# Rounding of two ternary weights in a feed-forward layer: one engine for both, or VectorE for the first and GpSimd for the second

## The chip, the cores and the metric

The kernel runs on one core of a Trainium2 chip as one program on five engines: TensorE (PE), VectorE (DVE), ScalarE (ACT), GpSimd (POOL) and SyncE (SP, which here only starts DMAs). Times are device microseconds of one execution. The metric is the median of several executions; lower is better.

## The reference

Two layers of gated cross attention and feed-forward over x (2 x 512 tokens, width 512). The last of the four blocks is the one that matters here: a feed-forward block whose activations are rounded to 8 bits and whose two weights are rounded to the three values -1, 0 and 1, times a scale.

```python
def _weight_quant(w):
    scale = 1.0 / jnp.clip(jnp.mean(jnp.abs(w)), EPS, None)
    return jnp.clip(jnp.round(w * scale), -1.0, 1.0) / scale

def _bitlinear(x, w, b):                      # w1: 2048 x 512, w2: 512 x 2048
    return jnp.einsum('bsd,hd->bsh', _act_quant(x), _weight_quant(w)) + b

h = gelu(_bitlinear(x, w1, b1))
x = x + tanh(g_ffn[1]) * _bitlinear(h, w2, b2)
```

The mean is over the whole weight, so no piece of a weight can be rounded before all of it has been read and summed.

## The kernel before

The program is written out by hand: every stage appends a function to the list of each engine, an engine runs its functions in order, and engines meet only through semaphores. The stage of interest is `bit_ffn`, the last one, which starts when the second cross attention has added its last block to x.

Its setup has these steps. Both weights are loaded as float32 (`raw[0]`, `raw[1]`, each 128 partitions x 8192). ScalarE sums their absolute values (`sizes`, L2685). TensorE adds the sums over the partitions (L2738), and VectorE makes the mean and its inverse (`wmean`, `winv`, L2584 and L2586). Each weight is then treated in four pieces of 128 x 2048, CH = 4:

- two VectorE operations on a piece in place: times the inverse mean, at most 1 (L2592), and then at least -1, plus a large number that makes the addition round (MAGIC, L2594). The second waits for the first through a semaphore.
- one ScalarE operation, which takes MAGIC off and writes bfloat16 (L2694, into `wq`).

ScalarE takes the eight pieces in a fixed order, the four of the first weight and then the four of the second. After all eight it copies its share of the transposed weights: TensorE transposes both weights in 16 groups (L2753; eight groups per weight), and the groups are copied out of PSUM by ScalarE (even groups, L2678) and VectorE (odd groups, L2676) in turn. There are four PSUM buffers for groups, so TensorE's fifth group waits until ScalarE has copied the first. The groups of the first weight wait for its four rounded pieces (`s_wq` at CH), those of the second for all eight.

Behind that come, for each pair of token tiles, normalisation and rounding on VectorE, `hidden` (L2774), GELU, a second rounding, and the output matmuls (L2795). These wait for all 16 groups. GpSimd has nothing to do in this stage.

Of the kernel before, what the change touches and what calls it, by code (L numbers as in the profile page):

```python
# [14 lines left out]
ALU = mybir.AluOpType  # L15
ACT = mybir.ActivationFunctionType
# [32 lines left out]
def program(nc, a, out):  # L49
    ctx = ExitStack()  # L50
    with ctx:
        def sem(name):
            return ctx.enter_context(nc.semaphore(name))

        def keep(name, shape, dt=F32):
            return ctx.enter_context(nc.sbuf_tensor(name, shape, dt))
# [7 lines left out]
        ident = keep("ident", [P, P])  # L64
# [14 lines left out]
        programs = {"SP": [], "ACT": [], "PE": [], "DVE": [], "POOL": []}  # L79
# [89 lines left out]
        def sb(name, shape, dt=F32):  # L169
            return phase.enter_context(nc.sbuf_tensor(name, shape, dt))  # L170
# [2333 lines left out]
        def bit_ffn():  # L2504
# [4 lines left out]
            MAGIC = 1.5 * 2.0 ** 23  # L2509
            TOP, BOTTOM = 127.0, -128.0  # L2510
            GROUPS = 8
            raw = [sb("f_raw1", [P, HC, D]), sb("f_raw2", [P, KC, HID])]
            wq = [sb("f_wq1", [P, HC, D], BF16), sb("f_wq2", [P, KC, HID], BF16)]
            w1T, w2T = sb("f_w1T", [P, KC, HID], BF16), sb("f_w2T", [P, HC, D], BF16)
            identb, ones = sb("f_identb", [P, P], BF16), sb("f_ones", [P, P])
            size, wmean, winv = sb("f_size", [P, 2]), sb("f_wmean", [P, 2]), sb("f_winv", [P, 2])
# [13 lines left out]
            WTB = [pairs[2 + i // 2][:, (i % 2) * BANK:(i % 2 + 1) * BANK].bitcast(BF16) for i in range(4)]  # L2530

            s_w = [sem("f_w1"), sem("f_w2")]
            s_b, s_id, s_one = [sem(f"f_{n}") for n in ("b", "id", "one")]
            s_size, s_sum, s_mean, s_wc, s_wr, s_wq, s_wt, s_wa, s_wd = [
                sem(f"f_{n}") for n in ("size", "sum", "mean", "wc", "wr", "wq", "wt", "wa", "wd")]
            s_ch, s_r, s_q, s_tr, s_te, s_m1, s_z, s_g, s_m2, s_o, s_x2 = [
# [1 line left out]
            CH = 4  # L2538
# [20 lines left out]
            def chunk(t3, k):  # L2559
                n = t3.shape[1] // CH  # L2560
                return t3[:, k * n:(k + 1) * n, :]
# [13 lines left out]

            def vector(dve):
                dve.wait_ge(*x2_done)
                dve.memset(ones[:, :], 1.0).then_inc(s_one, 1)

                dve.memset(scrap[:, 36:37], 0.0).then_inc(s_z, HB)  # L2580
                dve.memset(scrap[:, 37:38], 0.0).then_inc(s_o, 2)

                dve.wait_ge(s_sum, 1)
                dve.tensor_scalar(wmean[:, :], HID_B[0][:, 0:2], 1.0 / (HID * D), LEAST, ALU.mult, ALU.max).then_inc(s_mean, 1)  # L2584
                dve.wait_ge(s_mean, 1)
                dve.reciprocal(winv[:, :], wmean[:, :]).then_inc(s_mean, 1)  # L2586
                dve.wait_ge(s_mean, 2)

                for w in range(2):
                    for k in range(CH):  # L2590
                        c = chunk(raw[w], k)
                        dve.tensor_scalar(c, c, winv[:, w:w + 1], 1.0, ALU.mult, ALU.min).then_inc(s_wc, 1)  # L2592
                        dve.wait_ge(s_wc, w * CH + k + 1)
                        dve.tensor_scalar(c, c, -1.0, MAGIC, ALU.max, ALU.add).then_inc(s_wr, 1)  # L2594
                for g in range(1, 2 * GROUPS, 2):
                    dve.wait_ge(s_wt, g + 1)
                    turned(dve, g)
                dve.wait_ge(s_rstd, 4)
                dve.wait_ge(s_b, 32)

                steps = 0

                def step(ins, i):

                    nonlocal steps
                    steps += 1
                    ins.then_inc(s_ch, 1)

                    dve.wait_ge(s_ch, steps if i is None else first("steps", i) + steps)

                def quantise(src, n, w, i):
                    m, q = most[:, n:n + 1], scale[:, n:n + 1]
                    step(dve.tensor_scalar(m, m, LEAST, None, ALU.max), i)
                    step(dve.reciprocal(q, m), i)
                    step(dve.tensor_scalar(q, q, TOP, None, ALU.mult), i)
                    step(dve.tensor_scalar(unscale[:, n:n + 1], m, 1.0 / TOP, wmean[:, w:w + 1], ALU.mult, ALU.mult), i)
                    step(dve.tensor_scalar(src, src, q, MAGIC, ALU.mult, ALU.add), i)
                    dve.tensor_scalar(src, src, MAGIC + TOP, MAGIC + BOTTOM, ALU.min, ALU.max).then_inc(s_r, 1)

                def tile(t):  # L2620

                    if isinstance(t, int):
                        return x3[:, t, :], mv[:, 2 * t:2 * t + 1], rstd[:, t:t + 1]
                    return x3[:, bass.ds(t, 1), :].rearrange("p t d -> p (t d)"), mv[:, bass.ds(t * 2, 1)], rstd[:, bass.ds(t, 1)]

                def norm(pair, i):
                    for s in range(2):
                        xt, mean, one_over = tile(pair * 2 + s)
                        step(dve.tensor_scalar(h[s][:, :], xt, mean, one_over, ALU.subtract, ALU.mult), i)
                        step(dve.tensor_reduce(most[:, s:s + 1], h[s][:, :], AX.X, ALU.max, apply_absolute_value=True), i)  # L2630
                        quantise(h[s][:, :], s, 0, i)

                def hidden(pair, s):
                    for k in range(HB):
                        dve.wait_ge(s_m1, 2 * HB * pair + HB * s + k + 1)
                        cols = slice(k * BANK, (k + 1) * BANK)
                        dve.scalar_tensor_tensor(z[s][:, cols], HID_B[k][:, :], unscale[:, s:s + 1], b1[:, cols],
                                                 ALU.mult, ALU.add).then_inc(s_z, 1)

                norm(0, None)  # L2640
                for s in range(2):
                    hidden(0, s)
                norm(1, None)

                def body(i):
                    nonlocal steps
                    steps = 0
                    for s in range(2):
                        dve.wait_ge(s_g, 2 * i + s + 1)
                        step(dve.tensor_reduce(most[:, 2 + s:3 + s], z[s][:, :], AX.X, ALU.max, apply_absolute_value=True), i)  # L2650
                        quantise(z[s][:, :], 2 + s, 1, i)
                    for s in range(2):
                        if ahead(i, 1):
                            dve.wait_ge(s_q, first("rounded", i) + s + 1)
                            hidden(i + 1, s)
                        dve.wait_ge(s_m2, 2 * i + s + 1)
                        dve.scalar_tensor_tensor(o[s][:, :], OUT_B[s][:, :], unscale[:, 2 + s:3 + s], b2[:, :],
                                                 ALU.mult, ALU.add).then_inc(s_o, 1)
                        dve.wait_ge(s_o, 2 * i + s + 3)
                        xt = tile(i * 2 + s)[0]  # L2660
                        dve.scalar_tensor_tensor(xt, o[s][:, :], tgate[:, 3:4], xt, ALU.mult, ALU.add).then_inc(s_x2, 1)
                    if ahead(i, 2):
                        norm(i + 2, i)

                iterations(dve, body)

            def turned(engine, g):

                src = WTB[g % 4][:, :]
                if g < GROUPS:  # L2670
                    dst = w1T[:, g // 2, (g % 2) * 8 * P:(g % 2 + 1) * 8 * P]
                else:
                    m = (g - GROUPS) * 2
                    dst, src = w2T[:, m:m + 2, :], src.rearrange("p (m d) -> p m d", m=2)
                if g % 2:
                    engine.tensor_copy(dst, src).then_inc(s_wd, 1)  # L2676
                else:
                    engine.activation(dst, src, ACT.Copy).then_inc(s_wa, 1)  # L2678
# [7 lines left out]

            def scalar(act):
                act.wait_ge(s_size, 2)
                act.activation(identb[:, :], ident[:, :], ACT.Copy).then_inc(s_id, 1)
                act.activation(scrap[:, 40:41], eps[:, 0:1], ACT.Copy).then_inc(s_te, 2)  # L2690
                for w in range(2):
                    for k in range(CH):
                        act.wait_ge(s_wr, w * CH + k + 1)
                        act.activation(chunk(wq[w], k), chunk(raw[w], k), ACT.Copy, bias=-MAGIC).then_inc(s_wq, 1)  # L2694
                for g in range(0, 2 * GROUPS, 2):
                    act.wait_ge(s_wt, g + 1)
# [36 lines left out]
                iterations(act, body)  # L2733

            def tensor(pe):
                pe.wait_ge(s_one, 1)
                pe.wait_ge(s_size, 2)
                pe.matmul(HID_B[0][:, 0:2], ones[:, :], size[:, :], start=True, stop=True).then_inc(s_sum, 1)  # L2738
                pe.wait_ge(s_id, 1)
                for g in range(2 * GROUPS):  # L2740
                    if g < GROUPS:
                        pe.wait_ge(s_wq, CH)
# [62 lines left out]
            programs["DVE"].append(vector)  # L2805
            programs["ACT"].append(scalar)
            programs["PE"].append(tensor)

        bit_ffn()
        phase.close()  # L2810

# [69 lines left out]
```

## Time and profile before

| | |
|---|---|
| median of three executions | 2995.21 us (2987.34 to 2997.44) |
| the profiled execution: its time | 2988.46 us |
| the profiled execution: span of the trace | 2986.4 us |
| busy share of the span: PE, DVE, ACT, POOL | 81%, 60%, 49%, 37% |
| the stage `bit_ffn` in the trace | 2792.8 us to the end |

Clock times below are microseconds from the start of the trace. The rows further down come from the profile's page and from views of the trace: time windows with the busy time of each engine, the chain of work that ended last, the timeline of one engine, the statistics of one line of code, and groups of instructions by shape.

### The profile page before, as it was taken

How to read it: one execution, taken by the hardware profiler on the slowest of the kernel's cores; microseconds unless marked ns; L12 is line 12 of the kernel's file. 1: busy time of each engine (PE TensorE's matmuls, PEld its weight loads, DVE VectorE, ACT ScalarE, POOL GpSimd, SP SyncE). 2: the span in 40 equal slices, each digit the busy share in tenths (PEclk: the TensorE clock that was granted, in tenths of full speed). 3: DMA queues.
4: the chain of work that ended last, by engine and by line, in shares of the span. 5: the costliest groups of instructions: out<-in, count | busy, mean ns of one | idle time of the engine just before them, and what ended most of it. 6: DMA issues, size and time to landing. Idle time of an engine off the chain costs nothing.

```text
span 2986.4 us, 46041 instructions
## 1 busy us (share of the span) xinstructions
PE 2409.3 (81%) x14781; PEld 2001.7 (67%) x14789; DVE 1789.4 (60%) x3820; ACT 1472.2 (49%) x3029; POOL 1093.7 (37%) x1483
## 2 busy tenths in 40 slices
PE   6999999999958988889974899898057488889355
PEld 3878787878747888888863888887045376767232
DVE  3555555555544666666644554554467587878576
ACT  3444444444435666666642333332035586777543
POOL 0232323232304444444422656554454354444000
PEclk9999999999978999999985999999579799999787
DMA  3000000000000000000003455453626642331100
GB/s 107 19 18 11 7 18 18 11 7 18 0 29 11 19 18 18 18 18 18 18 11 108 154 174 176 156 175 113 185 77 219 169 99 68 80 86 64 74 8 21
DMA packets 111034, 195.02 MB, mean 65 GB/s; under 512 B 18336, under 2 KB 54432, under 8 KB 109024
## 3 DMA queue, kind: packets, MB, share of 16 engines
q1 hardware_dynamic: 97392, 159.59, 17.3%
q0 software_dynamic: 6640, 21.76, 2.2%
q10 hardware_dynamic: 6912, 12.59, 1.1%
q8 instruction: 42, 0.69, 0.1%
q14 instruction: 48, 0.39, 0.0%
HBM read 149.87 MB, written 44.04 MB: 65 GB/s over the span
## 4 chain that ended last, share of the span: by engine, by line
PE 66%; DVE 13%; issue 8%; ACT 7%; POOL 2%; DMA 2%; SPq 1%; DVEq 0%; ACTq 0%; POOLq 0%
PE pair L1768 8%; PE pair L535 6%; PE pair L1784 5%; PE pair L1066 5%; PE pair L1116 4%; PE pair L563 4%; PE pair L2453 4%; PE pair L496 4%; PE pair L521 3%; PE pair L1138 3%; PE pair L2436 3%; PE pair L2465 2%; PE pair L1100 2%; PE pair L552 2%; PE pair L502 2%
## 5 line engine op out<-in xcount | busy, mean ns | idle before, releaser
L433 ACT ACTIVATE x_p<-x_p,x_least 128x1024 f32<-128x1024 f32 x128 | 147.2, 1150 | 307.7 <-DVE x_least L389 307.7
L1440 POOL TENSOR_TENSOR e_w<-e_raw,e_w 128x2048 fp32r<-128x2048 f32 x48 | 220.4, 4593 | 153.7 <-ACT e_w L1406 153.6
L373 DVE TENSOR_TENSOR x_pT<-pair,x_pT 128x512 fp32r<-128x512 f32 x256 | 164.3, 684 | 121.2 <-ACT x_pT L452 121.2
L1768 PE MATMUL pair<-m_h,e_w 128*128 128x320 f32 x1536 | 229.5, 310 | 2.7 <-POOL e_w L1440 2.7
L1768 PEld LDWEIGHTS pair<-m_h,e_w 128*128 128x128 f32 x1536 | 228.0, 189 | 4.5 <-issue 3.1
L467 POOL TENSOR_TENSOR x_carry<-x_rtotal 128x1 f32<-128x1 f32 x128 | 24.9, 195 | 558.3 <-DVE x_rtotal L366 558.3
L535 PE MATMUL pair<-x_pT,x_v 128*128 128x256 f32 x1536 | 208.3, 292 | 9.2 <-DVE x_pT L373 9.2
L2365 DVE TENSOR_REDUCE z_most<-pair 128x1 f32<-128x1008 f32 x128 | 153.9, 1203 | 95.7 <-PE pair L2475 78.9
L535 PEld LDWEIGHTS pair<-x_pT,x_v 128*128 128x128 f32 x1536 | 192.7, 193 | 26.4 <-issue 18.4
L563 PE MATMUL pair<-x_kT,x_qT 128*128 128x512 f32 x768 | 207.3, 405 | 0.0
L978 ACT ACTIVATE s_p<-s_p,s_least 128x128 f32<-128x128 f32 (+3 forms) x256 | 143.6, 561 | 123.4 <-DVE s_least L888 123.4
L1116 PE MATMUL pair<-s_pT,s_v 128*128 128x256 f32 (+1 forms) x1152 | 158.9, 284 | 47.6 <-DVE s_pT L865 47.6
L2401 ACT ACTIVATE z_p<-pair,z_most 128x1008 f32<-128x1008 f32 (+1 forms) x256 | 174.6, 697 | 40.8 <-DVE z_most L2366 40.8
L1116 PEld LDWEIGHTS pair<-s_pT,s_v 128*128 128x128 f32 x1152 | 153.3, 196 | 60.0 <-issue 30.8
L2436 PE MATMUL pair<-ident,z_p 128*128 128x128 f32 x1024 | 144.7, 281 | 51.7 <-DVE z_pT L2358 50.7
L2387 ACT ACTIVATE z_pT<-pair 128x512 fp32r<-128x512 f32 x256 | 141.6, 601 | 88.6 <-PE pair L2436 88.6
L2436 PEld LDWEIGHTS pair<-ident,z_p 128*128 128x128 f32 x1024 | 117.2, 143 | 90.7 <-DVE z_pT L2358 62.1
L1038 POOL TENSOR_TENSOR s_carry<-s_rtotal 128x1 f32<-128x1 f32 x256 | 50.1, 196 | 345.9 <-DVE s_rtotal L859 345.6
L2421 POOL TENSOR_SCALAR z_p<-z_p,z_rtotal 128x1008 f32<-128x1008 f32 (+1 forms) x256 | 175.1, 697 | 0.0
L865 DVE TENSOR_TENSOR s_pT<-pair,s_pT 128x128 fp32r<-128x128 f32 (+3 forms) x256 | 124.6, 487 | 81.6 <-ACT s_pT L964 81.5
L2358 DVE TENSOR_TENSOR z_pT<-pair,z_pT 128x512 fp32r<-128x512 f32 x256 | 162.8, 677 | 4.8 <-ACT z_pT L2387 3.9
L452 ACT ACTIVATE x_pT<-pair 128x512 fp32r<-128x512 f32 x256 | 138.2, 593 | 43.7 <-PE pair L521 43.7
(322 smaller groups left out, 6112.6 us busy)
## 6 DMA issues: line engine op xcount, KB each, us to landing
e_raw<-in_L_ffn_w SPq DMA_DIRECT2D x48, 1024.0 KB
y_rows<-hslot ACTq DMA_DIRECT2D x48, 256.0 KB, 4.6
z_v<-z_vst SPq DMA_DIRECT2D x16, 768.0 KB, 3.6
z_kS<-z_k SPq DMA_DIRECT2D x24, 512.0 KB, 10.4
z_vS<-z_v SPq DMA_DIRECT2D x8, 1536.0 KB, 6.7
f_raw<-in_L_ffn_w SPq DMA_DIRECT2D x2, 4096.0 KB, 13.5
z_qS<-z_q SPq DMA_DIRECT2D x24, 256.0 KB, 4.5
s_wraw<-in_L_ffn_wq SPq DMA_DIRECT2D x9, 512.0 KB, 4.3
```

The costliest lines, as they stand in the source:

```text
L373: dve.tensor_tensor(pT[1][:, keys, q * P:(q + 1) * P], TR[j][:, :].rearrange("p (k n) -> p k n", n=P), pT[0][:, keys, q * P:(q + 1) * P].b ...
L535: mm = pe.matmul(OB[:, cols], v[x0][b][:, k, :], pT[x1][:, k, cols], start=(half == 0 and n == 0 and k == 0), stop=(half == 1 and n == 2 a ...
L563: mm = pe.matmul(SC[n % 2][:, j * BANK:(j + 1) * BANK], qT[x0][b][n // QT][:, n % QT * P:(n % QT + 1) * P], kT[x1][b][:, j * BANK:(j + 1) ...
L1066: mm = pe.matmul(o[:, 0:PW], hTa[x0][:, c, rows], w[x1][:, c, :], start=(n == 0 and c == 0), stop=(n == 2 and c == KC - 1))
L1116: mm = pe.matmul(OB[:, cols], v[b][:, k, first:first + 2, :].rearrange("p k d -> p (k d)"), pT[x1][:, k, cols], start=(i % 2 == 0 and half ...
L1440: pool.tensor_tensor(dst[1][:, :, :], raw[parity][:, :, :], dst[0][:, :, :].bitcast(F32), ALU.subtract).then_inc(s_lo, 1)
L1768: mm = pe.matmul(GU[m % 2][:, j * BANK:j * BANK + CAP], w[x0][:, c, m * P:(m + 1) * P], XS[s][x1][:, c, :], start=(n == 0 and c == 0), sto ...
L2358: dve.tensor_tensor(pT[1][:, k, cols], TR[i][:, :].rearrange("p (k n) -> p k n", n=P), pT[0][:, k, cols].bitcast(F32), ALU.subtract).then_ ...
L2365: dve.tensor_reduce(most[:, w, 0:1], SC[n % 2][:, 0:MAIN], AX.X, ALU.max, negate=True)
L2401: act.activation(p[w][:, cols], SC[n % 2][:, cols], ACT.Exp, bias=most[:, w, k:k + 1], accum_out=total[:, w, k:k + 1]).then_inc(s_ex, 1)
L2421: pool.tensor_scalar(p[w][:, cols], p[w][:, cols], rtotal[:, w, k:k + 1], 1.0, ALU.mult, ALU.mult).then_inc(s_pn, 1)
L2436: mm = pe.transpose(TR[i][:, k * P:(k + 1) * P], p[n % RING][:, kk * P:(kk + 1) * P], ident[:, :])
```

## The change

VectorE keeps the two operations on the four pieces of the first weight. The same two operations on the four pieces of the second weight are given to GpSimd, in a new function at the end of its program, with two semaphores of its own (`s_pc` between the two operations of a piece, `s_pr` for ScalarE). GpSimd starts when the inverse means are there, which is when VectorE starts too. ScalarE's order of pieces stays; only the semaphore that it waits for differs for the last four.

Two semaphores are saved by counting on others: the memset of `ones` now counts on `s_mean` (whose later values grow by one), and ScalarE's copy of the identity counts on `s_size`.

```diff
-                dve.memset(ones[:, :], 1.0).then_inc(s_one, 1)
+                dve.memset(ones[:, :], 1.0).then_inc(s_mean, 1)
...
-                for w in range(2):
-                    for k in range(CH):
-                        c = chunk(raw[w], k)
-                        dve.tensor_scalar(c, c, winv[:, w:w + 1], 1.0, ALU.mult, ALU.min).then_inc(s_wc, 1)
-                        dve.wait_ge(s_wc, w * CH + k + 1)
-                        dve.tensor_scalar(c, c, -1.0, MAGIC, ALU.max, ALU.add).then_inc(s_wr, 1)
+                for k in range(CH):
+                    c = chunk(raw[0], k)
+                    dve.tensor_scalar(c, c, winv[:, 0:1], 1.0, ALU.mult, ALU.min).then_inc(s_wc, 1)
+                    dve.wait_ge(s_wc, k + 1)
+                    dve.tensor_scalar(c, c, -1.0, MAGIC, ALU.max, ALU.add).then_inc(s_wr, 1)
...
+            def gpsimd(pool):
+                pool.wait_ge(s_mean, 3)
+                for k in range(CH):
+                    c = chunk(raw[1], k)
+                    pool.tensor_scalar(c, c, winv[:, 1:2], 1.0, ALU.mult, ALU.min).then_inc(s_pc, 1)
+                    pool.wait_ge(s_pc, k + 1)
+                    pool.tensor_scalar(c, c, -1.0, MAGIC, ALU.max, ALU.add).then_inc(s_pr, 1)
...
-                        act.wait_ge(s_wr, w * CH + k + 1)
+                        act.wait_ge((s_wr, s_pr)[w], k + 1)
...
-                pe.wait_ge(s_one, 1)
+                pe.wait_ge(s_mean, 1)
...
-                pe.wait_ge(s_id, 1)
+                pe.wait_ge(s_size, 3)
...
+            programs["POOL"].append(gpsimd)
```

GpSimd's instructions at the end of its program, as a difference with what each waits for left out. The first two rows are the last of the cross attention stage; `f_raw` is `raw` and `f_winv` is `winv`.

```order
 L2421 TENSOR_SCALAR z_p<-z_p,z_rtotal 128x1008
 L2421 TENSOR_SCALAR z_p<-z_p,z_rtotal 128x16
+L2670 TENSOR_SCALAR f_raw<-f_raw,f_winv 128x2048
+L2672 TENSOR_SCALAR f_raw<-f_raw 128x2048
+L2670 TENSOR_SCALAR f_raw<-f_raw,f_winv 128x2048
+L2672 TENSOR_SCALAR f_raw<-f_raw 128x2048
+L2670 TENSOR_SCALAR f_raw<-f_raw,f_winv 128x2048
+L2672 TENSOR_SCALAR f_raw<-f_raw 128x2048
+L2670 TENSOR_SCALAR f_raw<-f_raw,f_winv 128x2048
+L2672 TENSOR_SCALAR f_raw<-f_raw 128x2048
```

Eight operations are added behind everything else that GpSimd does, and nothing stands behind them.

ScalarE's instructions from its sums to the first copies of transposed groups, before:

```order
1161 L2685 ACTIVATE f_wq,f_size<-f_raw 128x8192 [waits f_w1,x_wd]
1162 L2685 ACTIVATE f_wq,f_size<-f_raw 128x8192 [waits f_w2]
1163 L99 ACT_TABLE_LOAD [waits ln_mv]
1164 L99 ACTIVATE std<-mv,eps 128x8 [waits s_eps]
1165 L2689 ACTIVATE f_identb<-ident 128x128 [waits f_size]
1166 L2690 ACTIVATE scrap<-eps 128x1
1167 L2694 ACTIVATE f_wq<-f_raw 128x2048 [waits f_wr] x8
1168 L2678 ACTIVATE f_w1T<-pair 128x1024 [waits f_wt] x4
```

and the same place of the changed kernel:

```order
1161 L2692 ACTIVATE f_wq,f_size<-f_raw 128x8192 [waits f_w1,x_wd]
1162 L2692 ACTIVATE f_wq,f_size<-f_raw 128x8192 [waits f_w2]
1163 L99 ACT_TABLE_LOAD [waits ln_mv]
1164 L99 ACTIVATE std<-mv,eps 128x8 [waits s_eps]
1165 L2696 ACTIVATE f_identb<-ident 128x128 [waits f_size]
1166 L2697 ACTIVATE scrap<-eps 128x1
1167 L2701 ACTIVATE f_wq<-f_raw 128x2048 [waits f_wr] x4
1168 L2701 ACTIVATE f_wq<-f_raw 128x2048 [waits f_pr] x4
1169 L2685 ACTIVATE f_w1T<-pair 128x1024 [waits f_wt] x4
```

The eight conversions stand where they stood, ahead of the first copy of a transposed group; the last four now wait for GpSimd's semaphore.

## Rows read from the trace of the kernel before

**Rows 1.** Windows: each engine's busy time, clock granted to PE, DMA share.

```profile
core 0: us, PE busy (x) PEld busy (x) DVE busy (x) ACT busy (x) POOL busy (x), PEclk, DMA share, GB/s
2816.00:2836.00 20.00, 3.57 (x32) 3.33 (x32) 19.70 (x17) 13.57 (x8) 0.00 (x0) 0.50 0.00 0
2836.00:2847.00 11.00, 7.92 (x96) 7.77 (x96) 4.69 (x8) 9.14 (x9) 0.00 (x0) 0.65 0.00 0
2842.00:2846.00 4.00, 4.00 (x59) 3.99 (x57) 2.25 (x4) 3.10 (x4) 0.00 (x0) 0.78 0.00 0
```

**Rows 2.** The chain that ended last, from the rounding on: start, us, what.

```profile
2816.03 1.30 DVE f_raw L2592
2817.35 1.23 DVE f_raw L2594
...
2834.55 1.24 DVE f_raw L2594
2835.79 0.02 issue
2835.81 1.91 ACT f_wq L2694
2837.72 0.92 ACT f_w1T L2678
2838.64 0.14 issue
2838.78 1.23 PE pair L2753 x10
```

**Rows 3.** Timeline of the same stretch: start, us, instruction, [idle before and releaser].

```profile
2825.98 1.91 ACT L2694 ACTIVATE f_wq<-f_raw 128x2048 bf16<-128x2048 f32 x1 [0.55 <-DVE f_raw L2594]
2828.04 3.57 PE L2753 MATMUL pair<-f_identb,f_wq 128*128 128x128 bf16 x32 [12.44 <-ACT f_wq L2694]
2837.63 1.92 ACT L2678 ACTIVATE f_w1T<-pair 128x1024 bf16<-128x1024 bf16 x2
```

**Rows 4.** Statistics of the pieces' lines: ns min/median/max, first and last start.

```profile
L2592 DVE TENSOR_SCALAR f_raw<-f_raw,f_winv x8: 1279/1281/1285, 2816.0 to 2833.2; 128x2048 f32<-128x2048 f32 x8
L2594 DVE TENSOR_SCALAR f_raw<-f_raw x8: 1226/1227/1228, 2817.3 to 2834.6; 128x2048 f32<-128x2048 f32 x8
```

**Rows 5.** GpSimd's groups by shape: busy us, mean ns, idle before.

```profile
L1440 POOL TENSOR_TENSOR e_w<-e_raw,e_w 128x2048 fp32r<-128x2048 f32 x48 | 220.4, 4593 | 153.7 <-ACT e_w L1406 153.6
L468 POOL TENSOR_SCALAR x_p<-x_p,x_rtotal 128x1024 f32<-128x1024 f32 x128 | 144.0, 1125 | 0.0
L1039 POOL TENSOR_SCALAR s_p<-s_p,s_rtotal 128x512 f32<-128x512 f32 x64 | 44.9, 701 | 0.0
```

**Rows 6.** Timelines of DVE and of POOL, 2168 to 2182, second cross attention.

```profile
2169.00 3.35 DVE L2082 TENSOR_TENSOR z_wkvraw<-z_wkvraw,z_wmean 128x1024 f32<-128x1024 f32 x1
2174.64 4.94 DVE L2082 TENSOR_TENSOR z_bd<-z_bd,z_wmean 128x512 f32<-128x512 f32 x1
...
2168.92 2.35 POOL L2243 TENSOR_TENSOR z_wd<-z_wdraw,z_wd 128x1024 fp32r<-128x1024 f32 x1 [37.38 <-ACT z_wd L2169]
2171.23 3.34 POOL L2243 TENSOR_TENSOR z_wd<-z_wdraw,z_wd 128x1024 fp32r<-128x1024 f32 x1
2174.53 4.49 POOL L2250 TENSOR_TENSOR z_cT<-z_xThi,z_cT 128x2048 fp32r<-128x2048 f32 x1
```

**Rows 7.** One line's statistics, then timelines of DVE and POOL at 2247.

```profile
L2132 DVE TENSOR_SCALAR hslot<-x,mv,rstd x8: 534/1608/1612, 2242.4 to 2282.3; 128x512 f32<-128x512 f32 x8
...
2245.83 0.25 DVE L2156 RECIPROCAL z_rdev<-z_dev 128x16 f32<-128x16 f32 x1
2247.14 1.61 DVE L2132 TENSOR_SCALAR hslot<-x,mv,rstd 128x512 f32<-128x512 f32 x1
...
2246.16 1.05 POOL L2259 TENSOR_TENSOR z_kt<-z_kt,z_rdev 128x512 f32<-128x512 f32 x1 [4.24 <-DVE z_rdev L2156]
2247.17 1.30 POOL L2266 TENSOR_TENSOR z_vst<-z_vt,z_vst 128x512 fp32r<-128x512 f32 x1
```

**Rows 8.** Statistics of two lines, then timelines at 908.9, self attention's start.

```profile
L1021 POOL TENSOR_TENSOR s_rot<-s_raw,s_cos x64: 872/881/1164, 902.6 to 1477.8; 128x320 f32<-128x320 f32 x64
L814 DVE TENSOR_TENSOR s_turned<-s_raw,s_sin x2: 491/818/1146, 908.9 to 909.3; 128x320 f32<-128x320 f32 x2
...
908.90 1.55 DVE L814 TENSOR_TENSOR s_turned<-s_raw,s_sin 128x320 f32<-128x320 f32 x2 [2.56 <-ACT s_raw L928]
...
908.94 1.16 POOL L1021 TENSOR_TENSOR s_rot<-s_raw,s_cos 128x320 f32<-128x320 f32 x1 [1.23 <-ACT s_raw L928]
909.31 1.15 DVE L814 TENSOR_TENSOR s_turned<-s_raw,s_sin 128x320 f32<-128x320 f32 x1
```

More of the change, by code:

```diff
@@ L2532, in bit_ffn @@
             s_w = [sem("f_w1"), sem("f_w2")]
-            s_b, s_id, s_one = [sem(f"f_{n}") for n in ("b", "id", "one")]
+            s_b, s_pc, s_pr = [sem(f"f_{n}") for n in ("b", "pc", "pr")]
             s_size, s_sum, s_mean, s_wc, s_wr, s_wq, s_wt, s_wa, s_wd = [
@@ L2584, in vector @@
                 dve.tensor_scalar(wmean[:, :], HID_B[0][:, 0:2], 1.0 / (HID * D), LEAST, ALU.mult, ALU.max).then_inc(s_mean, 1)
-                dve.wait_ge(s_mean, 1)
+                dve.wait_ge(s_mean, 2)
                 dve.reciprocal(winv[:, :], wmean[:, :]).then_inc(s_mean, 1)
-                dve.wait_ge(s_mean, 2)
-                for w in range(2):
-                    for k in range(CH):
-                        c = chunk(raw[w], k)
-                        dve.tensor_scalar(c, c, winv[:, w:w + 1], 1.0, ALU.mult, ALU.min).then_inc(s_wc, 1)
-                        dve.wait_ge(s_wc, w * CH + k + 1)
-                        dve.tensor_scalar(c, c, -1.0, MAGIC, ALU.max, ALU.add).then_inc(s_wr, 1)
+                dve.wait_ge(s_mean, 3)
+                for k in range(CH):
[3 more added lines that the diff above has]
+                    dve.tensor_scalar(c, c, -1.0, MAGIC, ALU.max, ALU.add).then_inc(s_wr, 1)
                 for g in range(1, 2 * GROUPS, 2):
@@ L2688, in scalar @@
                 act.wait_ge(s_size, 2)
-                act.activation(identb[:, :], ident[:, :], ACT.Copy).then_inc(s_id, 1)
+                act.activation(identb[:, :], ident[:, :], ACT.Copy).then_inc(s_size, 1)
                 act.activation(scrap[:, 40:41], eps[:, 0:1], ACT.Copy).then_inc(s_te, 2)
```

## Prediction

> **What bounds the kernel now.** I read the windows first, to see which engine fills the stage that is edited. From 2816 to 2836 VectorE is busy 19.70 of 20 us, ScalarE 13.57, and GpSimd not at all [rows 1]. The chain of work that ended last says the same: it runs through VectorE's sixteen operations on the weights, from 2816.03 to 2835.79, then through ScalarE's eighth conversion (1.91 us, to 2837.72), its first copy of a transposed group, and TensorE's fifth group at 2838.78 [rows 2]. So every microsecond by which ScalarE's eighth conversion ends earlier or later moves the end of the kernel, as long as the copies and transposes behind it keep their spacing. They do: TensorE's first four groups need 3.57 us and wait at 2828.04 for the fourth conversion, long before ScalarE's first copy at 2837.63 [rows 3].
>
> The quantity to work out is therefore one number: when the eighth conversion ends, against 2837.72.
>
> **What is removed.** VectorE loses eight operations, four of 1.281 and four of 1.227 us [rows 4], half of the 19.76 us that the sixteen take on the chain.
>
> **What is added.** GpSimd gets eight operations of 128x2048. The trace has none of that size, and none with min, max or add in this form. Its operations of the same form with two multiplications take 701 ns for 512 columns and 1125 ns for 1024 [rows 5]: 424 ns for 512 columns, 0.83 ns a column, so 1125 + 848 = 1973 ns for 2048, an estimate. The upper bound is the two-input subtraction of 128x2048, 4593 ns [rows 5]. I take 1.97 us, since that row has the same form; ends for the range are 1.97 and 4.59.
>
> The Trainium skill (GPSIMD Engine Reference, section 3.1) gives 1.03 cycles a column, at 1.2 GHz, to bodies with up to two operations. By the page that is an estimate of 1.76 us for one operation, and the sum below would be about 1.7 us smaller.
>
> **What VectorE and GpSimd do to each other.** This decides the case. Three places in the trace have both at work on SBUF.
>
> At 2169 VectorE's 128x1024 operation starts 0.08 us behind one of GpSimd. It takes 3.35 us: it ends at 2172.35, 1.08 us after GpSimd's ends at 2171.27. GpSimd's next, of the same size as its first, takes 3.34 instead of 2.35 us, 0.99 more. At 2174.64 a 128x512 operation of VectorE starts beside a GpSimd operation that ends at 2179.02, and ends only 0.56 us after it [rows 6]. They don't slow each other in proportion: one stands still until the other has finished.
>
> The rounding operations are of another kind on VectorE, with one input; 2048 columns in 1.23 us is 0.60 ns a column [rows 4]. Such an operation at 2247 takes 1.61 us beside GpSimd, against 0.534 for the fastest of the eight, and ends at 2248.75, 0.28 after GpSimd's at 2248.47 [rows 7]. So this kind stands still too. There GpSimd went from one of its operations (to 2247.21) to the next at 2247.17 although VectorE's had started at 2247.14; it had stood for under 0.1 us.
>
> Who is served next? At 908.90 VectorE has two operations with no wait between them (491 and 1146 ns). GpSimd's arrives 0.04 us after the first. It takes 1.16 instead of 0.88 us, so it waited about 0.28, for the first one only; the second, started at 909.31, ends at 910.46, 0.36 after GpSimd's at 910.10 [rows 8]. The two at 2169 show it the other way round: VectorE's operation gets in between two of GpSimd [rows 6]. The engine that has stood waiting for most of an operation gets the next turn, so two engines with full queues alternate strictly.
>
> **The sum.** Operation D0 of VectorE starts at 2816.03 [rows 2]. GpSimd starts about 0.08 us behind its releaser, as at 2246.16 after 2246.08 [rows 7], so VectorE is first. A VectorE operation of 1.23 to 1.28 us makes GpSimd wait about 0.99 us (the 1024-column case, whose 1.08 us after GpSimd's end is nearest to what I expect of one of these [rows 6]). GpSimd's consecutive starts are 0.04 us closer than its durations (2168.92 + 2.35 against 2171.23 [rows 6]). One turn of both is 1.97 - 0.04 + 0.99 = 2.92 us.
>
> - GpSimd's first ends at 2816.12 + 1.0 + 1.97 = 2819.1, its eighth 7 x 2.92 = 20.4 later, at 2839.5.
> - VectorE's eighth ends 1.1 us after GpSimd's seventh (2836.6), at 2837.7. The first weight, which now has only four pieces, is rounded later than both weights were before (2835.79).
> - ScalarE converts the first weight's last piece from 2837.7 to 2839.6. Only then does it come to the second weight, whose four pieces are ready by then: their starts are 1.82 us apart when nothing is waited for (2835.81 to 2837.63 [rows 2, 3]), so the eighth conversion starts at 2839.6 + 3 x 1.82 = 2845.1 and ends at 2847.0.
>
> Against 2837.72 that is +9.3 us. The profiled execution would go from 2988.46 (span 2986.4) to 2997.8. That execution lies 6.75 us under the median of the three, 2995.21, so I add the difference to the median: **3004.5 us**, +0.31%.
>
> The rest costs nothing. TensorE's first groups start at about 2839.6 instead of 2828.04, take 3.57 us, and are done before ScalarE's first copy at 2846.9; with a cover of 3.7 us gone they would cost what lies beyond. VectorE's odd copies of them come under the same cover. The merged semaphores count the same events. PE's clock is at 0.50 before these transposes and 0.78 in 2842 to 2846 [rows 1]; a shorter gap between the two bursts of transposes might let it rise earlier, worth under 1 us of the 7.92 [rows 1], which I leave out. GpSimd has nothing behind the eight, and no DMA moves.
>
> The Trainium skill (SBUF — State Buffer, section "Who interferes with whom") says that GpSimd and such VectorE operations share a port pair under an exclusive lock, held for a whole instruction. The trace agrees, with 1.61 against 0.534 us; it speaks against this change, since work that alternates is a sum, and not a maximum.
>
> **Rivals.**
>
> *GpSimd's operations are slower with min, max and add (30%).* The turn grows by what they take over 1.97. With 4.59: the eighth ends at 2816.12 + 1.0 + 4.59 + 7 x 5.54 = 2860.5; ScalarE, after VectorE's last at 2856 or so, converts at 2857, 2859, 2861, 2863 and 2865, and ends at about 2866.5: +28.8, 3024. For it: the same engine needs 2.24 ns a column for the subtraction [rows 5]. Against: that one reads two tensors, this one reads one.
>
> *VectorE gets two in a row where no wait lies between them (13%).* Then the order is D0, G0, D1 D2, G1, D3 D4, G2, D5 D6, G3, D7 and four of GpSimd alone. VectorE is done at about 2832.3, GpSimd at 2840.0, and the last conversion ends at 2841.9: +4.2, 2999.4, no measurable change. Against: the two at 908.90 were parted [rows 8].
>
> *No exclusion between operations of these kinds (8%).* This is the case on the other side of no change. VectorE's pieces keep their spacing, ScalarE ends the fourth at 2827.89 (2825.98 + 1.91 [rows 3]), GpSimd ends its eighth at 2816.1 + 8 x 1.93 = 2831.6, so ScalarE runs through: 2827.8 + 3 x 1.82 + 1.91 = 2835.2, -2.5 us, 2992.7. More than that can't be gained, since ScalarE's conversions then bound the stage. It decides once the two overlap for over half of the time. Against: 0.534 against 1.61 us [rows 7].
>
> *Anything else (7%):* a different first turn, or a shift elsewhere by timing alone.
>
> **How the numbers follow.** Strict alternation at 1.97 us has 42%, and gives the time predicted, 3004.5. The range, 2996 to 3025, takes in the doubled turns below and the slow GpSimd operations above; it leaves out no exclusion and the tails. 0.3% is 9.0 us, about what a measurement of this kernel tells from no change, and the likeliest case lies on that line: I count half of its 42% as slower, with the 30% of the slow GpSimd operations and 2% of the rest: slower 0.53. Same: 21 + 13 + 8 + 2 = 0.44. Faster 0.03.
>
> **What would show it.** In the changed profile, VectorE's eight operations should take about 3.0 us each but the first, and GpSimd's eight 2.9 to 3.0; their ends should alternate; ScalarE's fifth conversion should start near 2839.6, right behind its fourth, and its eighth end near 2847. The prediction is wrong if VectorE's operations keep 1.23 to 1.28 us, if GpSimd's take well over 3 us, or if TensorE's fifth group is not moved by the shift of the eighth conversion.

## The result and the profile after

The changed kernel takes 3037.74 us (median of four, 3034.66 to 3039.0) against 2992.03 us (four executions, 2987.34 to 2997.44): a ratio of 1.0151, 95% interval 1.0129 to 1.0172. It is 45.7 us slower. The forecast was 9.3 us slower, with a range that ended at 3025.

GpSimd's timeline of the changed kernel, from the moment when the inverse means are there (start, duration, instruction):

```profile
2816.51 8.26 POOL L2670 TENSOR_SCALAR f_raw<-f_raw,f_winv 128x2048 f32<-128x2048 f32 x1 [43.25 <-DVE f_winv L2586]
2824.85 7.94 POOL L2672 TENSOR_SCALAR f_raw<-f_raw 128x2048 f32<-128x2048 f32 x1
2832.78 8.11 POOL L2670 TENSOR_SCALAR f_raw<-f_raw,f_winv 128x2048 f32<-128x2048 f32 x1
...
2873.21 7.93 POOL L2672 TENSOR_SCALAR f_raw<-f_raw 128x2048 f32<-128x2048 f32 x1
```

The chain of work that ended last, same stretch (start, us, what), answers to [rows 2]:

```profile
2816.45 1.30 DVE f_raw L2591
2817.75 0.02 issue
2817.77 8.08 DVE f_raw L2593
2825.85 8.03 DVE f_raw L2591
...
2866.14 8.08 DVE f_raw L2593
2874.21 0.02 issue
2874.24 9.11 ACT f_wq L2701 x5
2883.34 0.92 ACT f_w1T L2685
2884.26 0.14 issue
2884.39 1.65 PE pair L2760 x14
```

Two things are to be seen. The order is the one that was forecast: VectorE's first operation runs alone in 1.30 us, and each further one ends about a microsecond after one of GpSimd's (2824.77, then 2825.85); the first weight's fourth piece comes late; and ScalarE then runs five conversions in one go. But a turn of both engines is 8.06 us, not 2.92. The eighth conversion ends at 2883.35, 66.9 us after VectorE's first start, where before it was 21.7 (2837.72 less 2816.03 [rows 2]). These 45.2 us are the loss, and nearly all of it; from VectorE's first start to the end of the trace it is 216.15 against 170.37 us, 45.8 more.

The statistics of the four lines, where [rows 4] had 1281 and 1227 ns:

```profile
L2591 DVE TENSOR_SCALAR f_raw<-f_raw,f_winv x4: 1286/8096/8100, 2816.4 to 2858.0; 128x2048 f32<-128x2048 f32 x4
L2670 POOL TENSOR_SCALAR f_raw<-f_raw,f_winv x4: 8107/8107/8256, 2816.5 to 2865.0; 128x2048 f32<-128x2048 f32 x4
L2593 DVE TENSOR_SCALAR f_raw<-f_raw x4: 8065/8066/8077, 2817.8 to 2866.1; 128x2048 f32<-128x2048 f32 x4
L2672 POOL TENSOR_SCALAR f_raw<-f_raw x4: 7929/7930/7939, 2824.8 to 2873.2; 128x2048 f32<-128x2048 f32 x4
```

They read as if both engines had become slow. One has, as the second experiment below shows: the other's durations hold its standing still.

### The profile page after: what moved, and what is told of

The parts are those of the page before. It is cut to its first block, busy times and chain, and to the rows that moved or that the text cites. A ratio compares the mean times of both kernels' runs of the same rounds, so it can differ in the third digit from the quotient of the medians.

```text
span 3032.6 us, 46049 instructions
## 1 busy us (share of the span) xinstructions
PE 2410.8 (79%) x14789; PEld 2002.2 (66%) x14789; DVE 1829.0 (60%) x3812; ACT 1471.3 (49%) x3029; POOL 1153.6 (38%) x1491
## 4 chain that ended last, share of the span: by engine, by line
PE 65%; DVE 15%; issue 8%; ACT 7%; DMA 2%; POOL 2%; SPq 1%; DVEq 0%; ACTq 0%; POOLq 0%
PE pair L1768 7%; PE pair L535 6%; PE pair L1784 5%; PE pair L1066 5%; PE pair L563 4%; PE pair L1116 4%; PE pair L2453 4%; PE pair L496 4%; PE pair L521 3%; PE pair L1138 3%; PE pair L2436 3%; PE pair L2465 2%; PE pair L1100 2%; PE pair L552 2%; PE pair L502 2%
## 5 line engine op out<-in xcount | busy, mean ns | idle before, releaser
L452 ACT ACTIVATE x_pT<-pair 128x512 fp32r<-128x512 f32 x256 | 138.2, 594 | 45.2 <-PE pair L521 45.2
```

## The experiments

Three theories could explain 8 us for a GpSimd operation. The diffs below leave lines out at "...". **K**: the pair of arithmetic operations decides, and those with min, max and add go a slow way. **C**: VectorE's operations beside it slow GpSimd down. **S**: 2048 columns are slow whatever the kind.

### Only the kinds changed

This kernel leaves out the rounding of the second weight.

```diff
-                    pool.tensor_scalar(c, c, winv[:, 1:2], 1.0, ALU.mult, ALU.min).then_inc(s_pc, 1)
+                    pool.tensor_scalar(c, c, winv[:, 1:2], 1.0, ALU.mult, ALU.mult).then_inc(s_pc, 1)
...
-                    pool.tensor_scalar(c, c, -1.0, MAGIC, ALU.max, ALU.add).then_inc(s_pr, 1)
+                    pool.tensor_scalar(c, c, 1.0, 1.0, ALU.mult, ALU.mult).then_inc(s_pr, 1)
```

> GpSimd's eight operations in the changed kernel are all two multiplications (first by the inverse mean and 1.0, second by 1.0 and 1.0), so the second weight is scaled but not rounded; shape, place and order are unchanged. Theory K (the kinds of operations decide): each takes about 1.97 us alone and 2.96 us with its wait for VectorE, VectorE's from the second on about 3.0 us, the eighth conversion of ScalarE ends near 2847 and the time is 9 to 10 us over that of before. Theory C (VectorE's operations beside it slow GpSimd) and theory S (2048 columns are slow in any kind): GpSimd's stay at 8 us and the time stays about 45 us over.

Measured: ratio 1.0043 (1.0029 to 1.0057), 3000.2 against 2987.94 us. GpSimd's timeline:

```profile
2816.82 3.06 POOL L2670 TENSOR_SCALAR f_raw<-f_raw,f_winv 128x2048 f32<-128x2048 f32 x1 [42.98 <-DVE f_winv L2586]
2819.97 2.74 POOL L2672 TENSOR_SCALAR f_raw<-f_raw 128x2048 f32<-128x2048 f32 x1
2822.69 2.93 POOL L2670 TENSOR_SCALAR f_raw<-f_raw,f_winv 128x2048 f32<-128x2048 f32 x1
```

and ScalarE's last stretch of conversions:

```profile
2838.21 9.11 ACT L2701 ACTIVATE f_wq<-f_raw 128x2048 bf16<-128x2048 f32 x5 [3.83 <-DVE f_raw L2593]
```

The eighth conversion ends at 2847.32, 30.6 us after VectorE's first start (2816.76). The prediction's sum, made for 1.97 us an operation, had 2847.0 less 2816.03, or 31.0. So with fast operations the rest of the sum holds; shape, size and the company of VectorE are the same as in the changed kernel, which speaks against C and S. (To the end of the trace the loss is 7.2 us, 177.5 against 170.4 from VectorE's first start, where the stage loses 8.9: what follows the stage differs by a microsecond or two between traces.)

### The two engines kept apart

```diff
                 pool.wait_ge(s_mean, 3)
+                pool.wait_ge(s_wr, CH)
```

> GpSimd starts its eight operations only when VectorE has done its eight, so the two never overlap. Theory K: VectorE's take 1.23 to 1.28 us, GpSimd's 7.1 and 6.9 us (8.11 and 7.93 less the 1.0 us of VectorE's turn), so the last conversion ends at about 2826 + 56 + 2 = 2884, and the time is within 2 us of that of the changed kernel, 46 us over before: the taking of turns costs almost nothing there. Theory C: GpSimd's take about 2 us, the last conversion ends near 2844 and the time is 6 us over before.

Measured: ratio 1.0162 (1.0144 to 1.0181), 3037.73 us, the same as the changed kernel. VectorE's last operation and GpSimd's first two:

```profile
2828.58 1.23 DVE L2593 TENSOR_SCALAR f_raw<-f_raw 128x2048 f32<-128x2048 f32 x1
```

```profile
2829.97 7.16 POOL L2671 TENSOR_SCALAR f_raw<-f_raw,f_winv 128x2048 f32<-128x2048 f32 x1 [53.02 <-DVE f_raw L2593]
2837.22 7.09 POOL L2673 TENSOR_SCALAR f_raw<-f_raw 128x2048 f32<-128x2048 f32 x1
```

VectorE is back at its old durations, and GpSimd takes 7.16 and 7.09 us with no rounding on VectorE beside it. Theory C is out. Of the 8.11 us in the changed kernel, 0.95 were VectorE's turn.

ScalarE's eighth conversion:

```profile
2887.33 1.91 ACT L2702 ACTIVATE f_wq<-f_raw 128x2048 bf16<-128x2048 f32 x1 [12.42 <-POOL f_raw L2673]
```

It ends 69.4 us after VectorE's first start (2819.88). Side by side it was 66.9, so with slow kinds the overlap is worth 2.5 us of the stage, though the two medians don't tell the kernels apart.

### Kinds of operation, one by one

Behind the last block of x, on a weight that nobody reads any more, each operation waits for the one before:

```diff
+                pool.wait_ge(s_x2, NT)
+                c, c5, one = raw[1][:, 0, :], raw[1][:, 0, 0:512], ones[:, 0:1]
...
+                one_more(pool.tensor_scalar(c, c, one, 1.0, ALU.mult, ALU.mult))
+                one_more(pool.tensor_scalar(c, c, one, 1.0e30, ALU.mult, ALU.min))
+                one_more(pool.tensor_scalar(c, c, -1.0e30, 0.0, ALU.max, ALU.add))
...
```

> The kernel before with the merged semaphores, and, when the last block of x is done, 14 GpSimd operations one after another on a weight that nobody reads any more: eleven kinds of 128x2048 and three of 128x512. The time is longer by their sum. Theory K: two multiplications take 1.97 us, (mult, min) 7.1, (max, add) 6.9; the others tell which kinds are slow; at 512 columns (mult, mult) takes 0.70 us and (mult, min) 1.7 to 1.9. Theory S: all of 2048 columns are alike at 7 us, and those of 512 are alike at 0.7 us. Theory C: all of 2048 columns are alike at 2 us.

Measured in one execution of 3054.51 us, GpSimd's timeline. The lines are in this order: L2814 (mult, mult), L2815 (mult, min), L2816 (max, add), L2817 (mult, max), L2818 (mult, add), L2820 (add, add), L2821 (min, max), L2822 one multiplication alone; L2825 (mult, mult) and L2826 (mult, min) on 512 columns.

```profile
2987.21 1.97 POOL L2814 TENSOR_SCALAR f_raw<-f_raw,f_ones 128x2048 f32<-128x2048 f32 x1 [209.06 <-DVE x L2661]
2989.28 7.16 POOL L2815 TENSOR_SCALAR f_raw<-f_raw,f_ones 128x2048 f32<-128x2048 f32 x1
2996.53 7.09 POOL L2816 TENSOR_SCALAR f_raw<-f_raw 128x2048 f32<-128x2048 f32 x1
3003.71 7.17 POOL L2817 TENSOR_SCALAR f_raw<-f_raw,f_ones 128x2048 f32<-128x2048 f32 x1
3010.97 1.97 POOL L2818 TENSOR_SCALAR f_raw<-f_raw,f_ones 128x2048 f32<-128x2048 f32 x1
...
3015.02 7.10 POOL L2820 TENSOR_SCALAR f_raw<-f_raw 128x2048 f32<-128x2048 f32 x1
3022.20 1.89 POOL L2821 TENSOR_SCALAR f_raw<-f_raw 128x2048 f32<-128x2048 f32 x1
3024.19 5.45 POOL L2822 TENSOR_SCALAR f_raw<-f_raw,f_ones 128x2048 f32<-128x2048 f32 x1
...
3040.64 0.69 POOL L2825 TENSOR_SCALAR f_raw<-f_raw,f_ones 128x512 f32<-128x512 f32 x1
3041.43 2.00 POOL L2826 TENSOR_SCALAR f_raw<-f_raw,f_ones 128x512 f32<-128x512 f32 x1
```

Theory K stands, and S is out: 512 columns show the same split. The constants aren't the cause: (mult, min) takes 7.16 us here with 1.0e30 on ones, and 7.16 in the run before this one with 1.0 on the real scale. The slow way costs (7.16 - 2.00) / 1536 = 3.36 ns a column, the fast one (1.97 - 0.69) / 1536 = 0.83. The two kinds that the change uses are both slow. No run shows why a pair is slow.

### More kinds

> As e3_pool_kinds, with eight other kinds of GpSimd operation on 128x2048 behind the last block of x. The theory is now that a few pairs have a fast form (1.9 to 2.0 us, as mult-mult, mult-add, min-max) and every other pair goes a slow way (7.1 us). If what counts is which two operations are paired, in either order, (add, mult) and (max, min) are fast; if the order counts, they take 7.1 us. (subtract, mult) and (mult, subtract) are open; (add, min), (min, min) and (min, add) are expected at 7.1; a plain copy at 1.9 or less.

Measured in one execution of 3036.32 us, in the order L2814 (add, mult), L2815 (max, min), L2816 (subtract, mult), L2817 (mult, subtract), L2819 (min, min), L2821 a plain copy:

```profile
2979.83 1.90 POOL L2814 TENSOR_SCALAR f_raw<-f_raw 128x2048 f32<-128x2048 f32 x1 [208.75 <-DVE x L2661]
2981.82 7.08 POOL L2815 TENSOR_SCALAR f_raw<-f_raw 128x2048 f32<-128x2048 f32 x1
2988.98 7.11 POOL L2816 TENSOR_SCALAR f_raw<-f_raw 128x2048 f32<-128x2048 f32 x1
2996.19 7.17 POOL L2817 TENSOR_SCALAR f_raw<-f_raw,f_ones 128x2048 f32<-128x2048 f32 x1
...
3010.62 7.08 POOL L2819 TENSOR_SCALAR f_raw<-f_raw 128x2048 f32<-128x2048 f32 x1
...
3024.93 1.89 POOL L2821 COPY f_raw<-f_raw 128x2048 f32<-128x2048 f32 x1
```

Neither of the two simple rules holds: (add, mult) is fast as (mult, add) is, but (max, min) is slow where (min, max) is fast. Of fourteen pairs tried, four are fast: mult-mult, mult-add, add-mult and min-max. The other two pairs of this run, (add, min) and (min, add), took 7.10 and 7.08 us. Most pairs were timed once, in one execution; (mult, min) and (max, add) recur with the same durations in the second experiment, (mult, add) and (min, max) in the one with fast kinds kept apart.

### The same rounding in fast kinds

```diff
-                    pool.tensor_scalar(c, c, winv[:, 1:2], 1.0, ALU.mult, ALU.min).then_inc(s_pc, 1)
+                    pool.tensor_scalar(c, c, winv[:, 1:2], MAGIC, ALU.mult, ALU.add).then_inc(s_pc, 1)
...
-                    pool.tensor_scalar(c, c, -1.0, MAGIC, ALU.max, ALU.add).then_inc(s_pr, 1)
+                    pool.tensor_scalar(c, c, MAGIC + 1.0, MAGIC - 1.0, ALU.min, ALU.max).then_inc(s_pr, 1)
```

> The changed kernel, with GpSimd's two operations written with the kinds that took 1.97 and 1.89 us: times the inverse mean, plus MAGIC (mult, add), then at most MAGIC + 1, at least MAGIC - 1 (min, max). The values are those of the reference: rounded first, then clipped. Theory K with strict turns: GpSimd's operations 2.7 to 3.1 us, VectorE's 2.9, the eighth conversion ends 30.5 us after VectorE's first start (21.7 before, 66.9 in the changed kernel), and the time is 9 to 12 us over before, as with the two multiplications.

Measured: ratio 1.0029 (1.0018 to 1.004), 2997.11 against 2989.1 us. VectorE's first operation, GpSimd's last, and ScalarE's last five conversions:

```profile
2815.39 1.29 DVE L2591 TENSOR_SCALAR f_raw<-f_raw,f_winv 128x2048 f32<-128x2048 f32 x1
2835.83 2.74 POOL L2672 TENSOR_SCALAR f_raw<-f_raw 128x2048 f32<-128x2048 f32 x1
2836.85 9.11 ACT L2701 ACTIVATE f_wq<-f_raw 128x2048 bf16<-128x2048 f32 x5 [3.83 <-DVE f_raw L2593]
```

The eighth conversion ends 30.6 us after VectorE's first start (2845.96 less 2815.39). Rewriting two operations takes 36 of the 45 us off; what is left, 8.9 us in the stage, is what the prediction had worked out as 9.3.

### Fast kinds, the two engines kept apart

The edit is that of the second experiment, on top of the last one.

> As e5_fast_kinds, but GpSimd starts only when VectorE's eight operations are done: no overlap. If turns are exclusive, running the two side by side gains nothing over this: GpSimd's eight end at 9.9 + 8 x 2.0 = 26 us after VectorE's first start (24 when side by side), and since ScalarE converts the first weight meanwhile, the eighth conversion ends at 28, which is 2 to 3 us before that of e5_fast_kinds. Without exclusion it would end 7 us after it.

Measured: ratio 1.0021 (1.0011 to 1.0031), 2994.99 us. The eighth conversion ends 28.1 us after VectorE's first start, 2.5 us before that of the kernel in which both work at the same time:

```profile
2824.49 1.23 DVE L2593 TENSOR_SCALAR f_raw<-f_raw 128x2048 f32<-128x2048 f32 x1
```

```profile
2825.88 1.98 POOL L2671 TENSOR_SCALAR f_raw<-f_raw,f_winv 128x2048 f32<-128x2048 f32 x1 [53.24 <-DVE f_raw L2593]
...
2840.08 1.89 POOL L2673 TENSOR_SCALAR f_raw<-f_raw 128x2048 f32<-128x2048 f32 x1
```

```profile
2842.01 1.91 ACT L2702 ACTIVATE f_wq<-f_raw 128x2048 bf16<-128x2048 f32 x1 [2.14 <-POOL f_raw L2673]
```

Side by side is worse here than one behind the other, but not because the overlap gains nothing. It brings GpSimd's last operation forward, to 23.2 us after VectorE's first start (2838.57 less 2815.39) from 26.2 (2841.97 less 2815.80). But it holds up the first weight, which ScalarE needs first: five conversions then lie behind VectorE's last operation, where here a single one lies behind GpSimd's. With the slow kinds it was the other way round (66.9 side by side, 69.4 apart). It also shows what the 8.9 us of the last kernel are made of: 6.4 (28.1 less 21.7) remain without any overlap, since GpSimd needs 1.9 to 2.0 us where VectorE needed 1.2 to 1.3. Between the two ratios the intervals overlap; the difference is read from the stage.

### One piece for GpSimd

VectorE keeps seven pieces, GpSimd has the last one, in fast kinds. The loop is shown against that of the kernel before.

```diff
-                    for k in range(CH):
+                    for k in range(CH - w):
...
+                c = chunk(raw[1], CH - 1)
+                pool.tensor_scalar(c, c, winv[:, 1:2], MAGIC, ALU.mult, ALU.add).then_inc(s_pc, 1)
+                pool.wait_ge(s_pc, 1)
+                pool.tensor_scalar(c, c, MAGIC + 1.0, MAGIC - 1.0, ALU.min, ALU.max).then_inc(s_pr, 1)
```

> VectorE keeps seven pieces and GpSimd takes only the last piece of the second weight, in the fast kinds. If turns are exclusive, any operation given to GpSimd costs VectorE 1.9 us of standing still and saves it 1.23: its seventh piece is done 14 x 1.23 + 2 x 1.9 = 21.0 us after its start instead of 17.3, and the eighth conversion ends 21.0 + 1.9 + 1.8 = 24.7 us after VectorE's start, 3 us later than before. If there were no exclusion, ScalarE would end the eighth at 17.3 + 3.7 = 21.0, 0.7 us earlier than before. By time either is within 0.3% of before; the trace tells.

Measured: ratio 1.0005 (0.9995 to 1.0015). VectorE's timeline, and ScalarE's last two conversions:

```profile
2815.30 1.29 DVE L2592 TENSOR_SCALAR f_raw<-f_raw,f_winv 128x2048 f32<-128x2048 f32 x1
2816.62 2.88 DVE L2594 TENSOR_SCALAR f_raw<-f_raw 128x2048 f32<-128x2048 f32 x1
2819.43 2.90 DVE L2592 TENSOR_SCALAR f_raw<-f_raw,f_winv 128x2048 f32<-128x2048 f32 x1
2822.37 1.23 DVE L2594 TENSOR_SCALAR f_raw<-f_raw 128x2048 f32<-128x2048 f32 x1
...
2835.91 3.71 ACT L2701 ACTIVATE f_wq<-f_raw 128x2048 bf16<-128x2048 f32 x2 [0.55 <-DVE f_raw L2594]
```

Two of GpSimd's operations lengthen two of VectorE's, by 1.65 and 1.62 us, and the next is back at 1.23. The eighth conversion ends 24.3 us after the first start (2839.62 less 2815.30), 2.6 us later than before, not 0.7 earlier. Two operations cost VectorE 3.27 us of standing still, less than the 3.8 expected, and save it 2.51 (1.28 and 1.23). So VectorE's last one ends 0.8 us later (20.6 against 19.8 after the first start); the other 1.8 are a conversion, since ScalarE takes GpSimd's piece last and then has two left behind VectorE. By that price per operation no share pays while VectorE has operations waiting beside it. That is worked out from this run: one piece and four were run, and no other order of ScalarE's pieces.

### The merged semaphores alone

```diff
-                dve.memset(ones[:, :], 1.0).then_inc(s_one, 1)
+                dve.memset(ones[:, :], 1.0).then_inc(s_mean, 1)
...
-                pe.wait_ge(s_id, 1)
+                pe.wait_ge(s_size, 3)
```

> The kernel before with only the two merged semaphores; VectorE keeps all sixteen operations. All theories: no change beyond 0.3%, the eighth conversion ends within 0.5 us of 2837.7. If the merged counting had a part in the loss, it would show here as more than 1 us.

Measured: ratio 0.9998 (0.9988 to 1.0008). They cost nothing. The eighth conversion ends at 2838.72 and not within 0.5 us of 2837.7, but VectorE's first operation starts later too, at 2817.03; the distance is 21.7 us in both kernels. The shift comes from ahead of VectorE's first operation, whose start lies between 2815.30 and 2820.09 in the traces of this document.

### A version without GpSimd

The stage is shortened where it is long: ScalarE scales and rounds five of the pieces itself, and the conversions behind VectorE are gone. The diff is against the changed kernel.

```diff
+                act.wait_ge(s_mean, 3)
+                for w, k in TAKEN:
+                    act.activation(chunk(wq[w], k), chunk(raw[w], k), ACT.Identity, scale=winv[:, w:w + 1],
+                                   bias=offset[:, 0:1]).then_inc(s_wr, 1)
...
+                        dve.tensor_scalar(q, q, SMALL + 1.0, SMALL - 1.0, ALU.min, ALU.max).then_inc(s_wq, 1)
...
+                        dve.tensor_scalar(c, c, winv[:, w:w + 1], 1.0, ALU.mult, ALU.min).then_inc(s_wc, 1)
+                        dve.wait_ge(s_wc, own)
+                        dve.tensor_scalar(q, c, -1.0, SMALL, ALU.max, ALU.add).then_inc(s_wq, 1)
...
-                    engine.tensor_copy(dst, src).then_inc(s_wd, 1)
+                    engine.tensor_scalar(dst, src, -SMALL, None, ALU.add).then_inc(s_wd, 1)
```

> A version meant to beat both. The rounding is done by writing bfloat16 at 192 plus the value, where neighbours are 1 apart, and 192 is taken off where the transposed groups are copied out of PSUM. ScalarE scales and rounds five pieces by itself (1.9 us each), VectorE clips those in bfloat16 and does three pieces alone; GpSimd does nothing, and the eight conversions are gone. ScalarE is done after 5 x 1.85 = 9.3 us, VectorE after 6 x 1.25 + 5 clips of 0.7 to 1.2 us = 11 to 13.5 us, so the first copy by ScalarE of a transposed group starts near 9.5 us after VectorE's first start instead of 21.6, and TensorE's last groups wait for VectorE at 11 to 13.5: 8 to 11 us faster than before, ratio 0.996 to 0.9975. If ScalarE's scaled form is slower than its plain one, or the copies with the subtraction are, it is less.

Measured: ratio 0.9947 (0.9933 to 0.996), 2975.25 against 2989.1 us. VectorE's first clip in bfloat16, ScalarE's five pieces, and its first copies of transposed groups:

```profile
2822.55 0.69 DVE L2599 TENSOR_SCALAR f_wq<-f_wq 128x2048 bf16<-128x2048 bf16 x1
```

```profile
2820.09 10.04 ACT L2703 ACTIVATE f_wq<-f_raw,f_offset,f_winv 128x2048 bf16<-128x2048 f32 x5 [1.17 <-DVE f_winv L2590]
2830.03 1.91 ACT L2688 ACTIVATE f_w1T<-pair 128x1024 bf16<-128x1024 bf16 x2
```

The first copy starts 9.9 us after VectorE's first operation (2820.09), where before it was 21.6 (2837.63 less 2816.03 [rows 2, 3]): 11.7 us. Its trace is 12.0 us shorter from that operation to the end (158.4 against 170.4). The timed difference is 13.9 us between the medians, and its interval reaches from 12 to 20, so the 12.0 us of the trace lie at its lower end; whether there is more behind it is not settled. Either is more than the 8 to 11 us expected. It beats both kernels. The run changes several things at once (who rounds, how many passes, where the constant is taken off), so it doesn't tell what each is worth.

## Why the prediction was wrong

**The bound, the chain and what follows it** were right. The quantity to work out was the end of ScalarE's eighth conversion. It moved by 45.2 us, and the trace from VectorE's first start to the end by 45.8.

**Strict turns** were right, in order and in size. VectorE stands still while GpSimd works, ends 1.1 us after it, and takes 0.84 to 0.95 us from it, where the sum had 0.99. With fast operations the sum gave 31.0 us from the first start to the eighth conversion, and two kernels gave 30.6. The likeliest case's 9.3 us are the 8.9 that its stage then loses.

**The step that failed** is "I take 1.97 us, since that row has the same form". The row's form was the same (one input, two operations) and its kinds were not: mult-mult takes the fast way, at 0.83 ns a column, and the two kinds of the change take 7.16 and 7.09 us. The extrapolation over the size was exact, 1973 ns against 1.97 us measured. Put 7.12 in the place of 1.97 and leave the rest of the sum: seven GpSimd operations lie ahead of VectorE's eighth, each 5.15 us longer, which is 36.1 us, and with the 9.3 it makes 45.4. Measured are 45.2 in the stage.

**The upper bound failed too.** It was taken from the subtraction of two tensors, 4593 ns, a GpSimd row of that size, though its form was another. The slow kinds with one input need 7.1 us, more than that with two. The rival named for it (30%) had the right mechanism, slower operations in strict turns, and put its price at 28.8 us (by the prediction's own spacing of 1.82 us a conversion, 27.5); min, max and add aren't slow as such, since (min, max) and (mult, add) are fast. The Trainium skill's rule for bodies with up to two operations (GPSIMD Engine Reference, section 3.1) would give 1.76 us, an estimate; here 1.89 to 1.97 was measured for four pairs and 7.1 for the others, and the measurement decides. The prediction had the sum 1.7 us smaller by that rule; with seven GpSimd operations ahead of VectorE's eighth it is 1.5.

**No exclusion**, the rival on the other side, was wrong: one piece for GpSimd lengthens two of VectorE's operations by 1.6 us each. **Two in a row for VectorE** was wrong: every one of VectorE's after the first is long.

**What was costed at nothing** did cost nothing: the merged semaphores (0.9998). TensorE's first 32 transposes take 3.57 us behind the cover, as before. Whether PE's clock rises earlier after a shorter gap stays open: the 96 transposes behind the gap took 7.92 us before (gap 7.17 us), and with a gap of 4.53 us they took 8.26 in the changed kernel and 7.03 in the first experiment.

## What to carry to other kernels

A duration holds for the instruction and for the arithmetic that it does: before work is given to GpSimd, look for a row with the same pair of operations, and if there is none, time it once at the end of the kernel, where it costs one run. Then ask whether both engines' operations can run at once at all. If VectorE's stretch beside them in the trace, giving GpSimd a part is nearly a sum and not a maximum: a turn of both took 2.87 us with fast kinds (six turns of GpSimd's starts, 2818.60 to 2835.83), where GpSimd alone needs 2.03 and VectorE alone 1.24. An engine that doesn't stand still beside VectorE can be the better helper, here ScalarE. And where three engines work one behind the other, look first at whether a pass can go altogether.

## What the hardware showed that I had not expected

GpSimd's operations with one input of 128x2048 float32, in place, and two scalars fall in two classes in these runs. Multiply-multiply, multiply-add, add-multiply and min-max take 1.89 to 1.97 us, as a plain copy does (1.89). Multiply-min, max-add, multiply-max, add-add, max-min, subtract-multiply, multiply-subtract, add-min, min-min and min-add take 7.08 to 7.17. A single operation is in between, 5.45 us for a multiplication, so that multiplying twice, once by 1.0, is nearly three times as fast as multiplying once.
